# The gate's weights stay in TensorE while 512 tokens stream past, in a capacity-routed expert layer

## The reference, cut to what matters

```python
def _L1_ffn_ref(x, Wr, W1, W2):       # x: 8 x 512 tokens of 256; 8 experts; F = 1024; cap = 512
    probs = softmax(xf @ Wr)          # xf: layer-normalised tokens, 4096 x 256; Wr: 256 x 8
    eidx = argmax(probs)              # one expert a token
    rank = how many earlier tokens chose the same expert
    keep = rank < cap
    # expert e gets its first 512 tokens, in order:
    ye = relu(xe @ W1[e]) @ W2[e] * p_token
    x = x + y                         # tokens beyond the capacity stay as they are
```

## Time and profile before

| | us |
|---|---|
| median of 3 runs | 3147.78 (3138.3 to 3150.32) |
| the profiled execution | 3154.33 |
| its span | 3152.6 |
| TensorE busy | 2641.4 (84%) |
| VectorE busy | 1917.5 (61%) |
| ScalarE busy | 1497.7 (48%) |
| GpSimd busy | 783.3 (25%) |

### The profile page before, as it was taken

The page is one execution under the profiler, slowest core; times in us unless marked ns, Lnnn a source line. Parts: engine busy times, 40 slices in busy tenths (PEclk is TensorE's granted clock), DMA queues, the critical chain, the costliest instruction groups (busy, mean ns, idle before and its releaser), DMA issues. The chain is left out here.

```text
span 3152.6 us, 40374 instructions
## 1 busy us (share of the span) xinstructions
PE 2641.4 (84%) x12988; PEld 1372.0 (44%) x12988; DVE 1917.5 (61%) x5004; ACT 1497.7 (48%) x2912; POOL 783.3 (25%) x742
## 2 busy tenths in 40 slices
PE   4769999997565999999756688699789999985998
PEld 2324444444452343333345466466423333325666
DVE  4858888885528788888452444222388888853221
ACT  2447776776423766666632332111146777661110
POOL 0303332320322433222031300311133344304111
PEclk7789999999776999999977898699879999995999
DMA  7565555551254233322124103133242233304231
GB/s 241 166 210 160 159 159 158 162 162 46 80 152 137 92 101 105 98 82 92 46 84 149 47 1 112 63 119 120 86 141 92 92 101 110 103 16 165 80 117 53
DMA packets 216760, 351.41 MB, mean 111 GB/s; under 512 B 21465, under 2 KB 172636, under 8 KB 211816
## 3 DMA queue, kind: packets, MB, share of 16 engines
q1 hardware_dynamic: 201080, 299.42, 30.4%
q0 software_dynamic: 15472, 49.41, 4.5%
HBM read 199.51 MB, written 159.45 MB: 114 GB/s over the span
## 5 line engine op out<-in xcount | busy, mean ns | idle before, releaser
L1600 DVE CUSTOM_DVE_ANT_0 decay_junk<-decay_scores_q,decay_corr 128x512 bf16<-128x512 f32 x512 | 338.5, 684 | 121.0 <-PE decay_scores_q L1339 119.1
L1517 ACT ACTIVATE decay_probs<-decay_scores_k 128x512 f32<-128x512 f32 x512 | 294.7, 597 | 209.6 <-PE decay_scores_k L1358 171.8
L1603 DVE TENSOR_REDUCE rope_mx<-rope_scores_q 128x1 f32<-128x512 f32 x512 | 333.9, 685 | 90.5 <-PE rope_scores_q L1339 90.1
L1517 ACT ACTIVATE rope_probs<-rope_scores_k 128x512 f32<-128x512 f32 x512 | 294.6, 600 | 167.1 <-PE rope_scores_k L1352 165.8
L1603 DVE TENSOR_REDUCE latent_mx<-latent_scores_q 128x1 f32<-128x512 f32 x512 | 330.2, 683 | 69.4 <-PE latent_scores_q L1339 69.0
L1517 ACT ACTIVATE latent_probs<-latent_scores_k 128x512 f32<-128x512 f32 x512 | 295.0, 600 | 151.4 <-PE latent_scores_k L1352 149.5
L1339 PE MATMUL decay_scores_q<-decay_KS,decay_QS 96*128 96x512 bf16 x512 | 205.0, 401 | 47.4 <-DVE decay_mx L1600 34.7
L1339 PE MATMUL rope_scores_q<-rope_KS,rope_QS 96*128 96x512 bf16 x512 | 201.3, 395 | 21.5 <-DVE rope_mx L1603 12.0
L1339 PE MATMUL latent_scores_q<-latent_KS,latent_QS 96*128 96x512 bf16 x512 | 201.0, 395 | 20.4 <-DMA latent_QS<-latent_parts_dram 11.4
L1352 PE MATMUL latent_scores_k<-latent_QS,latent_KS 99*128 99x512 bf16 x512 | 197.0, 386 | 6.2 <-ACT latent_probs L1517 3.7
L1352 PE MATMUL rope_scores_k<-rope_QS,rope_KS 99*128 99x512 bf16 x512 | 197.2, 387 | 4.5 <-ACT rope_probs L1517 2.7
(11 more groups left out here) (396 smaller groups left out, 5315.1 us busy)
## 6 DMA issues: line engine op xcount, KB each, us to landing
decay_parts_dram<-decay_parts SPq DMA_DIRECT2D x64, 384.0 KB, 3.0
decay_KS<-decay_parts_dram SPq DMA_DIRECT2D x64, 384.0 KB, 6.3
decay_QS<-decay_parts_dram SPq DMA_DIRECT2D x64, 384.0 KB, 6.9
decay_parts_dram<-decay_parts SPq DMA_DIRECT2D x64, 256.0 KB, 3.1
experts3x_w<-in_w_dram SPq DMA_DIRECT2D x16, 1024.0 KB, 7.1
experts4x_w<-in_w_dram SPq DMA_DIRECT2D x16, 1024.0 KB, 7.0
experts_xin<-dispatched SPq DMA_DIRECT2D x96, 128.0 KB, 2.6
results<-experts_y SPq DMA_DIRECT2D x96, 128.0 KB, 2.1
```

Of the source, the lines that this page charges most:

```text
L1517: act.activation(probs[:, (b * 16 + kk) % PSLOTS, h, :], psB[:, s % 2, :], ACT.Exp, scale=scale).then_inc(exp_done, 1)
L1600: dve.tensor_tensor_reduce(junk[:, a % 2, :], psA[:, A_BANK[k], :], corr[:, qt, :], 1.0, -3.0e38, ALU.mult, ALU.max, mx[:, grp % 2, qt, h: ...
L1603: dve.tensor_reduce(mx[:, grp % 2, qt, h:h + 1], psA[:, A_BANK[k], :], AX.X, ALU.max).then_inc(a_done, 1)
```

## The change

`score(q)` now loads the gate's 128x8 halves as weights and streams all 512 turned tokens past each: two matmuls a batch, with a result of 8 partitions by 512 in psY. ACT copies it to a new SBUF tile lgT (`take_scores`). TensorE then turns it back with four transposes of 8x128 pieces (`turn_logits`) into psH, the PSUM tile that the expert stage uses later, and DVE's `logits` reads it there. The first matmul of the expert stage that writes psH therefore waits for the last logits copy.

The orders change too. TensorE's is now, for each q: turn q+1, count (q-3)/2 if q is odd and at least 3, score q, turn_logits q-1; at the end turn_logits 7 and count 3. DVE normalises three batches ahead and then, for each n: logits 2n, normalise 2n+3, logits 2n+1, one_hot n, normalise 2n+4, slots n. ACT's is, for each q: the two copies of batch q+1, the exponential of group (q-3)/2 if q is odd and at least 3, the copy of the scores of q; the exponential of group 3 comes last.

```diff
--- before.py
+++ after.py
@@ -442,6 +442,7 @@
         psR = ctx.enter_context(nc.psum_tensor(f"{g['layer']}x_ranks", [P, GT, E], F32))
         psC = ctx.enter_context(nc.psum_tensor(f"{g['layer']}x_totals", [P, GT, E], F32))
         wg, xnT = sb("wg", [P, 2, E], F32), sb("xnT", [P, 2, 2, S], F32)
+        lgT = sb("lgT", [E, 2, S], F32)
         lg, rk = sb("lg", [P, NT, E], F32), sb("rk", [P, GT, E], F32)
         over = sb("over", [P, GT, E], F32)
         ohb = sb("ohb", [P, GT, E], BF16)
@@ -455,6 +456,7 @@
         scattered, slots_ready = sem("scattered"), sem("slots_ready")
         gate_loaded, root, rstd_done, xn_ready = sem("gate_loaded"), sem("root"), sem("rstd_done"), sem("xn_ready")
         n_ready, n_taken = sem("normal_turned"), sem("normal_taken")
+        s_ready, s_taken = sem("scores_ready"), sem("scores_taken")
         l_ready, l_taken = sem("logits_ready"), sem("logits_taken")
         oh_ready, counted, steps = sem("one_hot_ready"), sem("counted"), sem("steps")
         shifted, exp_done, gated = sem("shifted"), sem("exp_done"), sem("gated")
@@ -525,11 +527,18 @@
             def score(q):
                 pe.wait_ge(n_taken, 2 * q + 2)
                 if q >= 2:
+                    pe.wait_ge(s_taken, q - 1)
+                for c in range(2):
+                    last = pe.matmul(psY[0:E, q % 2, :], wg[:, c, :], xnT[:, q % 2, c, :], start=(c == 0), stop=(c == 1))
+                last.then_inc(s_ready, 1)
+
+            def turn_logits(q):
+                pe.wait_ge(s_taken, q + 1)
+                if q >= 2:
                     pe.wait_ge(l_taken, q - 1)
                 for t in range(4):
-                    for c in range(2):
-                        last = pe.matmul(psY[:, q % 2, t * E:(t + 1) * E], xnT[:, q % 2, c, t * P:(t + 1) * P], wg[:, c, :],
-                                         start=(c == 0), stop=(c == 1))
+                    last = pe.transpose(psH[:, q % 2, t * E:(t + 1) * E], lgT[0:E, q % 2, t * P:(t + 1) * P],
+                                        g["ident"][0:E, 0:E])
                 last.then_inc(l_ready, 1)
 
             def count(n):
@@ -542,19 +551,16 @@
 
             pe.wait_ge(gate_loaded, 16)
             turn_normal(0)
-            turn_normal(1)
-            score(0)
-            turn_normal(2)
-            score(1)
-            score(2)
-            count(0)
-            for n in range(1, NT // GT):
-                turn_normal(2 * n + 1)
-                score(2 * n + 1)
-                if 2 * n + 2 < NB:
-                    turn_normal(2 * n + 2)
-                    score(2 * n + 2)
-                count(n)
+            for q in range(NB):
+                if q + 1 < NB:
+                    turn_normal(q + 1)
+                if q >= 3 and q % 2 == 1:
+                    count((q - 3) // 2)
+                score(q)
+                if q:
+                    turn_logits(q - 1)
+            turn_logits(NB - 1)
+            count(NT // GT - 1)
 
             def turn(j, p):
                 n = j * 2 + p
@@ -568,6 +574,8 @@
 
             def inner(j, p):
                 n = j * 2 + p
+                if n == 0:
+                    pe.wait_ge(l_taken, NB)
                 pe.wait_ge(w_loaded[p], j * 32 + 32)
                 pe.wait_ge(t_taken, n * 2 + 2)
                 for f in range(FC):
@@ -580,8 +588,6 @@
 
             def outer(j, p):
                 n = j * 2 + p
-                if n == 0:
-                    pe.wait_ge(l_taken, NB)
                 pe.wait_ge(h_even, n * (FC // 2) + FC // 2)
                 pe.wait_ge(h_odd, n * (FC // 2) + FC // 2)
                 for t in range(QT):
@@ -616,14 +622,26 @@
                 act.wait_ge(shifted, n + 1)
                 act.activation(over[:, :, :], over[:, :, :], ACT.Exp).then_inc(exp_done, 1)
 
-            for q in range(NB):
+            def take_normal(q):
                 for c in range(2):
                     act.wait_ge(n_ready, 2 * q + (c + 1))
                     if c == 0 and q >= 2:
-                        act.wait_ge(l_ready, q - 1)
+                        act.wait_ge(s_ready, q - 1)
                     act.copy(xnT[:, q % 2, c, :], psT[:, c, :]).then_inc(n_taken, 1)
-                if q and q % 2 == 0:
-                    exps(q // 2 - 1)
+
+            def take_scores(q):
+                act.wait_ge(s_ready, q + 1)
+                if q >= 2:
+                    act.wait_ge(l_ready, q - 1)
+                act.copy(lgT[0:E, q % 2, :], psY[0:E, q % 2, :]).then_inc(s_taken, 1)
+
+            take_normal(0)
+            for q in range(NB):
+                if q + 1 < NB:
+                    take_normal(q + 1)
+                if q >= 3 and q % 2 == 1:
+                    exps((q - 3) // 2)
+                take_scores(q)
             exps(NT // GT - 1)
 
             def take(j, p):
@@ -677,7 +695,7 @@
 
             def logits(q):
                 dve.wait_ge(l_ready, q + 1)
-                dve.tensor_copy(lg[:, 4 * q:4 * q + 4, :], psY[:, q % 2, 0:4 * E].rearrange("p (t e) -> p t e", t=4)).then_inc(
+                dve.tensor_copy(lg[:, 4 * q:4 * q + 4, :], psH[:, q % 2, 0:4 * E].rearrange("p (t e) -> p t e", t=4)).then_inc(
                     l_taken, 1)
 
             def one_hot(n):
@@ -723,16 +741,15 @@
             dve.wait_ge(rstd_done, 1)
             normalise(0)
             normalise(1)
-            logits(0)
+            normalise(2)
             for n in range(NT // GT):
-                if n:
-                    logits(2 * n)
-                if 2 * n + 2 < NB:
-                    normalise(2 * n + 2)
+                logits(2 * n)
+                if 2 * n + 3 < NB:
+                    normalise(2 * n + 3)
                 logits(2 * n + 1)
                 one_hot(n)
-                if 2 * n + 3 < NB:
-                    normalise(2 * n + 3)
+                if 2 * n + 4 < NB:
+                    normalise(2 * n + 4)
                 slots(n)
 
             def normal_tokens(e):
```

## The result

| | before | after |
|---|---|---|
| median, same chip, 7 runs each | 3145.88 (3138.3 to 3150.32) | 3160.55 (3152.93 to 3168.06) |
| the profiled execution | 3154.33 | 3165.74 |
| its span | 3152.6 | 3164.0 |

The ratio is 1.0052, 95% interval 1.0036 to 1.0068: 16 us slower, between 11 and 21. The forecast was 3166, 3150 to 3183. The busy shares hardly moved, as the page of the profile after shows, so the comparison has to be made in the routing stage.

What follows compares the result with a forecast made beforehand. TensorE's pace through the batches was taken to set group 2's places, and POOL's scatters the rest. Half the half-clock excess, 8 to 9 us a layer, plus 0.5, gave +18 over two layers: 3166 us against the 3147.8 median, range 3150 to 3183.

Steps and rivals of the forecast that it cites:

- The mechanism: Routing stage: TensorE idles before turns until DVE makes XN, 1.75 us behind logits, 3.2 with one_hot between.
- Rival B: Routing stage, set up for the experiments: new scores, turned logits and ACT's copy cost more in themselves; no chance given.
- The swap of the scores: TensorE, each batch: four 512-column instructions, 3.43 us at half clock, 1.72 at full, replace 3.44 us of old scores.
- The table load: ACT, before the first exponential: a load of 1.28 us, formerly hidden in a wait, now covered by nothing.
- the full-clock sum: Routing stage at full clock: places at 22.6, 35.6, 45.0, 50.0; group 1 binds, POOL ends at 67.2 against 66.9.
- the two sums: Routing stage worked out at half clock (POOL's end 83.9, 17 us a layer lost) and at full (67.2, nothing lost).
- The mixed case: Routing stage: clock rises in most pairs, falls in many DVE gaps; +8 to +28 us, at +18; chance 0.6.
- The low-clock rival: Routing stage: 8-column-wide scores are weak activity, so the clock stays low; +32 to +34 us, 3181; chance 0.22.
- The high-clock rival: Routing stage: clock stays high from the first scores on; 0 to +3 us, 3148 to 3151; chance 0.15.
- half-clock excess: Routing stage: loss of 17 us a layer if the clock stays low; the forecast took half, 8 to 9 us.
- The 0.5: Routing stage: 0.5 us a layer added for delays like an unexplained turn of 2.46 us instead of 1.8.
- The "faster" case: Routing stage: gain beyond 0.5%, needing POOL as only bound and first places by 17.1; chance 0.03.

Runs made afterwards that it cites:

- x9: The changed kernel with DVE making XN two batches further ahead of the logits, rerun on a chip without late signals; ratio 0.9973 to the kernel before.
- x2: The kernel before with the changed kernel's orders on TensorE, ACT and DVE but the old scores, no turning back; ratio 1.0008 to the kernel before.
- x4: The changed kernel with a throw-away exponential on ACT right behind the square root, loading the table early; ratio 1.0042 to the kernel before.
- x7: The changed kernel with 16 or 30 throw-away bf16 matmuls on TensorE ahead of each turn from batch 3 on; ratio 1.0032 to the kernel before.
- x1: The changed kernel with DVE making XN two batches further ahead of the logits, on a chip with late signals; ratio 1.0021 to the kernel before.
- x6: The kernel before with the changed kernel's orders and XN two batches further ahead, but the old scores; ratio 1.0028 to the kernel before.
- x3: The changed kernel's scores, copy and turning back in the old orders, each score followed at once by its turn back; ratio 1.0042 to the kernel before.
- x8: x1's kernel with POOL waiting for all four groups' places before its first scatter; one run, 3101.61 us beside 3074.8 for the kernel before.

## Why the prediction was right, and which sizes were off

- **The mechanism.** TensorE waits for XN behind logits, and behind logits and one_hot. Forecast 1.75 and 3.2 us; measured 1.57 and 3.21. (The working for 3.2, 1.73 + 1.38 + 0.2, adds to 3.3; the hand-overs took 0.1.) The 3.48 us ahead of turn 5 are behind slots 0, as forecast, but its sum leaves only 2.4 us there (31.7 to 34.1): the score before it ran mostly at the full clock, and TensorE came to the wait sooner. The 3.70 ahead of turn 6 (forecast 3.4) are logits and one_hot again (1.99) and an XN of 1.61 in place of 1.38. x9 takes these waits away by DVE's order alone, keeps the new scores, and turns +0.62% into -0.27%. Rival B falls with that.
- **What x2 adds.** The prediction put the cost on "the order". More exactly it is the order together with logits that trail by one score; with the old scores the same order waits a third as long. What the order costs by itself is in the first places, 4.1 us later at the half clock (25.2 against 21.1).
- **The swap of the scores.** Forecast 3.43 us at the half clock and 1.72 at the full: 3.42 (2853.49 to 2856.91) and 1.81 (2848.63 to 2850.44). Turned logits were over-estimated: 0.57 to 0.59 at the half clock and 0.41 at the full against 0.87 and 0.44, a term of 0.3 us a batch. ACT's copy is 0.575 against 0.59.
- **The table load.** It was forecast uncovered, at 1.28; x4 gives 1.4 and 2.0 for the first places and 1.5 at POOL's end.
- **Which group binds.** With after's mixed clock it is group 1, as in the full-clock sum: places at 43.6, plus 0.8, plus 24 x 1.285 is 75.2; measured 75.0. Its places lie between the two sums (35.6 and 49.3), and so do the first (22.6, 27.4, 32.5).
- **The clock.** The mixed case held: 0.72 and 0.73 over the stage against 0.50 before, full after a turn and a score back to back, low again behind the gaps of 3 us and more and, after one turn, behind the first of 1.57. The low-clock rival would have needed 0.50 throughout. The high-clock rival failed on the waits; with them gone the matmuls run at the full clock (1.88 us for four) up to 2785 in x9. By the Trainium skill ("TensorE: Matmul & The Clock Gate", Part 4) the transposes do not count for the clock; no run of mine separates turns from scores. The stretch in the earlier trace rows that the prediction set against this is one of four like it in the two profiles of the kernel before, and the other three were not followed by a higher clock. The rows below are the other layer of the same profile: 16 transposes, and the clock at 0.50 for all that follows. So that argument was weak, and what turns do for the clock stays open.

```profile
1945.50:1949.00 3.50, 3.50 (x16) 3.14 (x17) 1.10 (x4) 1.74 (x3) 0.00 (x0) 0.50 1.01 421
1949.00:1997.00 48.00, 39.26 (x186) 37.07 (x184) 22.29 (x95) 9.54 (x19) 19.77 (x20) 0.50 0.57 185
```

- **The sum.** Forecast 8 to 9 us a layer, +0.5, so +18. Measured 6.9 and 8.1 on the first chip, 8.5 and 8.4 on the undisturbed one. That it came so close is in part luck: half of the half-clock excess was a guess between two sums, and that excess hangs on group 2 while group 1 bound. The 0.5 had the wrong sign: it was for a delay of the kernel before (the turn of 2.46 us in the earlier trace rows), and that is one of the late signals. Before has them on the first chip (ends at 68.4 and 66.9 against 66.5), after has none there. That took 2.3 us off the difference, a stretch at the full clock in the second layer (1.5 us earlier first places) set off against it. 1.0052 against 1.0062 fits, but the intervals overlap.
- **What was left out.** The prediction kept DVE's order as it was, so it had no case in which the turns don't wait and the clock stays up. With the first places at 20 and those of all four groups by 40, as in x9, POOL works through its 41.1 us without a gap. The "faster" case was written off because first places by 17.1 were wanted for 0.5%; x9 is faster by 0.3% with first places at 20, where the prediction had 21.3 as the earliest and at most 1 to 2 us a layer to gain.

## What to carry to other kernels

When a change makes a result come out one step later in a pipeline, look at what stands behind that result in the consumer's program order: here the next input stood there, and the producer waited for it. Make inputs as many steps ahead as the buffers allow before judging the change itself; here a few lines of DVE's order decided between 0.6% slower and 0.3% faster. A gap costs more than its length when the clock falls behind it: the fills in x7, which leave the waits, gave back half of the loss. And read the gain against the bound behind it: with POOL's 41 us of scatters next in line, TensorE's time was worth only what brings the first and second groups' places forward.

## What the chip showed that was not expected

- **Late signals.** Where the kernel before takes 3146 to 3155 us, the end of TensorE's work is seen late by ACT and DVE while POOL issues scatters: 13.6 and 15.5 us in x1's two layers, up to 9.4 in x6, 7 in x3 and 5.9 in x2, 0.7 to 1.5 us twice a layer in the kernel before, none in after or x4. On the two chips where the kernel before takes 3074 us there was none in any of seven runs. For one and the same kernel (x1, x9) POOL's end moves from 61.7 and 62.1 to 70.5 and 69.7, 16.4 us, and the ratio from 0.9973 to 1.0021, 0.5%. In x1 the wait ended 0.6 us after POOL ran out of scatters, in its other layer 2.2; in x2 it ended while POOL was still issuing them. That POOL's scatters cause it was only argued: x8 was to test it and met a chip without late signals. What tells the chips apart stays open, and so do the 70 to 80 us between them: the routing stage of after takes the same 75 us on both kinds, and the kernel before is already 77.6 us apart when the first of the two changed layers starts (first XN at 1943.93 and 1866.38) and 78.3 at the second.
- **So the best version depends on the chip**: XN ahead is 0.3% faster than the kernel before where signals are prompt, and 0.2% slower on the one chip with late ones that it ran on. Its ratio is below after's on both kinds.
